# Edge attention on one Trainium2 core: the three logit products of a group on one column tile or on three

## What is computed

```
q, v = node_h @ Wq.T + bq, node_h @ Wv.T + bv          # 6250 x 8 heads x 16
k    = edge_attr @ Wk.T + bk                           # 100000 x 8 x 16
qs, qd = q[src], q[dst]
in_m, out_m, diag_m = sum(qs*k), sum(qd*k), sum(qs*qd) # over the 16 of a head
att   = distance ** lam
score = (seg_softmax(in_m/4, dst) + seg_softmax(out_m/4, dst) + seg_softmax(diag_m/4, dst)) * att
h     = segment_sum(score * v[dst], dst)
out   = leaky_relu(h @ Wo.T + bo, 0.1)
```

## Time and profile before

| | before |
|---|---|
| median of 3 runs | 7518.55 us (7517.9 to 7519.48) |
| the profiled execution | 7519.79 us |
| its span in the trace | 7518.0 us |
| PE busy | 5718.0 us (76%) |
| POOL busy | 5039.7 us (67%) |
| DVE busy | 3806.6 us (51%) |
| ACT busy | 1181.4 us (16%) |
| first and last logit product | 4785.2 and 6232.5 us |

### The profile page before, as it was taken

How to read it: one execution, slowest core, us unless ns; L and a number is a source line. 1 busy time by engine, 2 the same in 40 slices (tenths; PEclk the granted TensorE clock), 3 DMA queues, 4 the chain that set the end, 5 groups by cost and what they waited for, 6 DMA issues and landing times.

```text
span 7518.0 us, 99962 instructions
## 1 busy us (share of the span) xinstructions
PE 5718.0 (76%) x30467; PEld 3476.1 (46%) x30467; DVE 3806.6 (51%) x12655; ACT 1181.4 (16%) x3122; POOL 5039.7 (67%) x5069
## 2 busy tenths in 40 slices
PE   0677777777777777777577777899999995677776
PEld 0444444444444444444344444455555553444444
DVE  8834444444444444444544444577777777433335
ACT  0600000000000000000100000466666664000000
POOL 7077777677777677777577776466666661677774
PEclk9599999999999999999899999999999997999999
DMA  1021111211111211111111111354555450111111
GB/s 49 20 62 53 53 53 53 60 53 53 53 53 53 60 54 53 53 53 53 55 53 53 53 53 48 100 124 120 124 125 122 122 124 20 55 53 53 53 53 51
DMA packets 393953, 491.18 MB, mean 65 GB/s; under 512 B 104941, under 2 KB 291215, under 8 KB 393403
## 3 DMA queue, kind: packets, MB, share of 16 engines
q0 software_dynamic: 160528, 330.23, 15.7%
q1 hardware_dynamic: 229723, 153.27, 8.2%
q10 hardware_dynamic: 3168, 1.31, 0.1%
HBM read 459.92 MB, written 26.88 MB: 65 GB/s over the span
## 4 chain that ended last, share of the span: by engine, by line
POOL 52%; PE 22%; issue 17%; DVE 6%; ACT 1%; DMA 1%; ACTq 0%; DVEq 0%; POOLq 0%; SPq 0%
POOL pool L623 52%; PE psum L790 8%; PE psum L813 3%; PE psum L779 3%; PE psum L772 2%; DVE pool L1217 2%; PE psum L656 1%; PE psum L765 1%; PE psum L758 1%; PE psum L801 1%; PE psum L736 1%; PE psum L722 0%; DVE hot L1309 0%; DVE work L1051 0%; ACT work L929 0%
## 5 line engine op out<-in xcount | busy, mean ns | idle before, releaser
L623 POOL DMA_INDIRECT pool<-table,src_col x4160 | 3933.6, 946 | 1440.4 <-issue 1265.9
L745 PE MATMUL psum<-busy_rows,iota_b 128*128 128x512 bf16 x12480 | 3393.0, 381 | 0.0
L747 PE MATMUL psum<-pool 128*128 128x128 f32 x8320 | 1714.3, 288 | 1380.4 <-DVE pool L1342 1380.4
L747 PEld LDWEIGHTS psum<-pool 128*128 128x128 f32 x8320 | 1503.7, 191 | 2346.8 <-DVE pool L1342 1894.2
L1342 DVE TENSOR_SCALAR pool<-iota_f,rel_col,ew_col 128x128 f32<-128x128 f32 x3328 | 1228.5, 374 | 2291.4 <-DMA pool<-table,src_col 2290.4
L745 PEld LDWEIGHTS psum<-busy_rows,iota_b 128*128 128x128 bf16 x12480 | 1235.2, 99 | 545.9 <-issue 9.0
L1353 DVE TENSOR_TENSOR work<-work,psum 128x128 f32 x4160 | 1190.1, 286 | 252.6 <-PE psum L747 224.2
L605 POOL DMA_INDIRECT gath<-table,src_col x832 | 909.4, 1093 | 535.7 <-PE psum L765 341.2
L942 ACT ACTIVATE pool<-psum 128x512 f32<-128x512 f32 (+1 forms) x130 | 72.1, 566 | 4278.8 <-PE psum L722 4278.7
L790 PE MATMUL psum<-pool,head_sum 128*32 128x512 f32 x1248 | 614.9, 602 | 0.0
L1342 DVE TENSOR_SCALAR pool<-iota_f,rel_col 128x128 f32<-128x128 f32 x832 | 238.5, 287 | 577.6 <-DMA pool<-table,src_col 577.0
(11 more groups left out here) (195 smaller groups left out, 3938.6 us busy)
## 6 DMA issues: line engine op xcount, KB each, us to landing
pool<-table,src_col POOLq DMA_INDIRECT x4160, 2.5
pool<-edge_attr SPq DMA_DIRECT2D x832, 64.0 KB
pool<-step_masks SPq DMA_DIRECT2D x208, 192.0 KB
pool<-rel_rows SPq DMA_DIRECT2D x208, 128.0 KB, 3.1
table<-work SPq DMA_DIRECT2D x60, 256.0 KB, 2.3
gath<-table,src_col POOLq DMA_INDIRECT x832, 3.3
table<-QV SPq DMA_DIRECT2D x12, 256.0 KB, 2.3
out<-X SPq DMA_DIRECT2D x12, 256.0 KB
```

The lines of the kernel that those rows point to most:

```text
L623: gp.indirect_dma_start(out=gath_ring[:, s % RING, :], out_offset=None, in_=source[:, :], in_offset=bass.IndirectOffsetOnAxis(ap=src_col[: ...
L745: pe.matmul(psum[:, SUM_BANKS, :], iota_b[:, :], busy_rows[:, :], start=True, stop=True)
L747: pe.matmul(psum[:, s % SUM_BANKS, 0:D], hot_ring[:, s % HOT_RING, :], gath_ring[:, s % RING, :], start=True, stop=True).then_inc(steps.pr ...
```

## The change

The three kinds go to three column tiles, at partitions 0, 32 and 64 of the bank, and the quarters to eight rows each inside every tile: quarter q has the columns 8q to 8q + 7 of `head_sum`, and the four groups of a round accumulate into the same 96 rows. `keys(g + 1)` stands behind all three products instead of before the third, and PE waits for all three prods before the first. The logits signal once a group. Everything that worked on 128 partitions of the softmax works on 96, the ends are turned 96 columns wide and copied as 288, and a round's masks come in twelve loads of eight partitions, not four of 32.

```diff
-        head_sum = sb("head_sum", [P, 3, 32])
+        head_sum = sb("head_sum", [P, 4, 32])
...
-        ends = take(2, 3 * P)
+        KINDS = 3
+        ROWS = 32 * KINDS
+        ends = take(2, 3 * ROWS)
...
                 for q in range(QUADS):
                     s0 = q * QS + r * GROUP
-                    sp.dma_start(masks[32 * q:32 * (q + 1), r % 2, :, :],
-                                 spread(step_masks[:, s0:s0 + GROUP, :].rearrange("k (a s) e -> a k (s e)", a=1), 0, 32)
-                                 ).then_inc(masks_here[r % 2], 16)
+                    rows = step_masks[:, s0:s0 + GROUP, :].rearrange("k (a s) e -> a k (s e)", a=1)
+                    for kind in range(KINDS):
+                        first = 32 * kind + HEADS * q
+                        sp.dma_start(masks[first:first + HEADS, r % 2, :, :],
+                                     spread(rows, 0, HEADS)).then_inc(masks_here[r % 2], 16)
...
-            for k in range(3):
-                part = head_sum[:, k, HEADS * k:HEADS * (k + 1)]
+            for q in range(QUADS):
+                part = head_sum[:, q, HEADS * q:HEADS * (q + 1)]
...
-                for n, k in enumerate((2, 0, 1)):
-                    if n == 2 and g + 1 < NG:
-                        keys(g + 1)
-                    pe.wait_ge(prods_made, 3 * g + n + 1)
-                    pe.matmul(psum[32 * q:32 * (q + 1), bank, :], head_sum[:, k, :], prod[:, k, :], start=(n == 0),
-                              stop=(n == 2), tile_position=(0, 32 * q)).then_inc(logits_added, 1)
+                pe.wait_ge(prods_made, KINDS * (g + 1))
+                for kind in range(KINDS):
+                    ins = pe.matmul(psum[32 * kind:32 * (kind + 1), bank, :], head_sum[:, q, :], prod[:, kind, :],
+                                    start=(q == 0), stop=(q == QUADS - 1), tile_position=(0, 32 * kind))
+                ins.then_inc(logits_added, 1)
+                if g + 1 < NG:
+                    keys(g + 1)
...
-                for k, run in enumerate((m_run[:, cur, 1:BANK + 1], den_run[:, cur, :], num_run[:, cur, :])):
-                    ins = pe.transpose(psum[:, B_END, k * P:(k + 1) * P], run[:, j * P:(j + 1) * P], ident[:, :])
+                for k, run in enumerate((m_run[0:ROWS, cur, 1:BANK + 1], den_run[0:ROWS, cur, :], num_run[0:ROWS, cur, :])):
+                    ins = pe.transpose(psum[:, B_END, k * ROWS:(k + 1) * ROWS], run[:, j * P:(j + 1) * P], ident[0:ROWS, 0:ROWS])
...
-                values = ends[:, two, :].rearrange("p (k q c) -> p k q c", k=3, q=QUADS)
+                values = ends[:, two, :].rearrange("p (k i q h) -> p k i q h", k=3, i=KINDS, q=QUADS)
...
-                    ins = pe.matmul(psum[:, B_SUM, q * ACCW:(q + 1) * ACCW].rearrange("p (k c) -> p k c", k=3),
-                                    hot[:, two * QUADS + q, :], values[:, :, q, 0:SOFT], start=True, stop=True)
+                    ins = pe.matmul(psum[:, B_SUM, q * ACCW:(q + 1) * ACCW].rearrange("p (k i h) -> p k i h", k=3, i=KINDS),
+                                    hot[:, two * QUADS + q, :], values[:, :, :, q, :], start=True, stop=True)
...
-                act.activation(ends[:, c % 2, :], psum[:, B_END, 0:3 * P], ACT.Copy).then_inc(ends_copied, 1)
+                act.activation(ends[:, c % 2, :], psum[:, B_END, 0:3 * ROWS], ACT.Copy).then_inc(ends_copied, 1)
...
-                    v.wait_ge(logits_added, 3 * g)
+                    v.wait_ge(logits_added, g)
...
-                    v.wait_ge(logits_added, 3 * QUADS * (r + 1))
-                    v.wait_ge(masks_here[cur], 64 * (r // 2 + 1))
-                    v.tensor_tensor(invalid, psum[:, B_LOGIT[cur], :], invalid, ALU.add).then_inc(logits_masked, 1)
+                    v.wait_ge(logits_added, QUADS * (r + 1))
+                    v.wait_ge(masks_here[cur], 16 * QUADS * KINDS * (r // 2 + 1))
+                    v.tensor_tensor(invalid, psum[0:ROWS, B_LOGIT[cur], :], invalid, ALU.add).then_inc(logits_masked, 1)
```

More of the change, by code:

```diff
@@ L818, in attention_tensor @@
             pe.wait_ge(runs_clear, 3)
-            pe.wait_ge(head_sum_made, 10)
+            pe.wait_ge(head_sum_made, 1 + 3 * QUADS)
             turn_group(0)
@@ L994, in softmax_exp @@
             def softmax_exp(r, part):
-                starts = masks[:, r % 2, 1, :]
+                starts = masks[0:ROWS, r % 2, 1, :]
                 if part == 1:
                     act.wait_ge(below_made, r + 1)
-                    act.activation(expo[:, 0, :], expo[:, 0, :], ACT.Exp).then_inc(exp_made, 1)
+                    act.activation(expo[0:ROWS, 0, :], expo[0:ROWS, 0, :], ACT.Exp).then_inc(exp_made, 1)
                 else:
@@ L1385, in softmax_part @@
                 cur, old = r % 2, 1 - r % 2
-                m_now, m_before = m_run[:, cur, 1:BANK + 1], m_run[:, cur, 0:BANK]
-                invalid, starts, factor = (masks[:, cur, k, :] for k in range(3))
+                m_now, m_before = m_run[0:ROWS, cur, 1:BANK + 1], m_run[0:ROWS, cur, 0:BANK]
+                invalid, starts, factor = (masks[0:ROWS, cur, k, :] for k in range(3))
                 if part == 0:
-                    v.wait_ge(logits_added, 3 * QUADS * (r + 1))
-                    v.wait_ge(masks_here[cur], 64 * (r // 2 + 1))
-                    v.tensor_tensor(invalid, psum[:, B_LOGIT[cur], :], invalid, ALU.add).then_inc(logits_masked, 1)
+                    v.wait_ge(logits_added, QUADS * (r + 1))
+                    v.wait_ge(masks_here[cur], 16 * QUADS * KINDS * (r // 2 + 1))
+                    v.tensor_tensor(invalid, psum[0:ROWS, B_LOGIT[cur], :], invalid, ALU.add).then_inc(logits_masked, 1)
                     if r >= 2:
                         v.wait_ge(runs_turned, GROUP * (r - 1))
-                    v.tensor_copy(m_run[:, cur, 0:1], m_run[:, old, BANK:BANK + 1]).then_inc(own.up(), 1)
+                    v.tensor_copy(m_run[0:ROWS, cur, 0:1], m_run[0:ROWS, old, BANK:BANK + 1]).then_inc(own.up(), 1)
                     settle(own.value)
                     v.wait_ge(logits_masked, r + 1)
-                    v.tensor_tensor_scan(m_now, starts, invalid, m_run[:, cur, 0:1], ALU.add, ALU.max).then_inc(own.up(), 1)
+                    v.tensor_tensor_scan(m_now, starts, invalid, m_run[0:ROWS, cur, 0:1], ALU.add, ALU.max).then_inc(own.up(), 1)
                     soft["m"] = own.value
@@ L1400, in softmax_part @@
                     settle(soft["m"])
-                    v.tensor_tensor(expo[:, 0, :], invalid, m_now, ALU.subtract).then_inc(below_made, 1)
+                    v.tensor_tensor(expo[0:ROWS, 0, :], invalid, m_now, ALU.subtract).then_inc(below_made, 1)
                     v.tensor_tensor(starts, m_before, starts, ALU.add).then_inc(own.up(), 1)
@@ L1407, in softmax_part @@
                     v.wait_ge(exp_made, r + 1)
-                    v.tensor_tensor(factor, expo[:, 0, :], factor, ALU.mult).then_inc(own.up(), 1)
+                    v.tensor_tensor(factor, expo[0:ROWS, 0, :], factor, ALU.mult).then_inc(own.up(), 1)
                     soft["weighted"] = own.value
@@ L1411, in softmax_part @@
                     v.wait_ge(carry_made, r + 1)
-                    v.tensor_tensor_scan(den_run[:, cur, :], starts, expo[:, 0, :], den_run[:, old, BANK - 1:BANK], ALU.mult,
+                    v.tensor_tensor_scan(den_run[0:ROWS, cur, :], starts, expo[0:ROWS, 0, :], den_run[0:ROWS, old, BANK - 1:BANK], ALU.mult,
                                          ALU.add).then_inc(own.up(), 1)
                     settle(soft["weighted"])
-                    v.tensor_tensor_scan(num_run[:, cur, :], starts, factor, num_run[:, old, BANK - 1:BANK], ALU.mult,
+                    v.tensor_tensor_scan(num_run[0:ROWS, cur, :], starts, factor, num_run[0:ROWS, old, BANK - 1:BANK], ALU.mult,
                                          ALU.add).then_inc(num_made, 1)
```

## The result

The changed kernel takes 7241.21 us, the median of 4 runs (7238.71 to 7244.49), the kernel before 7518.9 beside it: 0.9631 of it, 95% interval 0.9614 to 0.9648. It is faster by 278 us. The forecast, 7293, is 52 us above it; the range, 7215 to 7475, holds it, and rival A's 7230 is the nearest of the recorded times.

The account below looks back on a forecast made before the run. PE was taken to bound the attention at 7.00 us a group, falling to 5.88: 199 x (7.00 - 5.88) = 223, and 4 for the first nine groups, 227 us off 7519.8 gives 7293 us; range 7215 to 7475.

Parts of the forecast that it names:

- rival A: Logit products: three tiles fully overlap, 0.97 us; POOL then binds at 5.61 us a group; 7230 us, chance 0.12.
- main term: Logit products on three column tiles: 2.80 us down to 1.83, saving 0.97 us a group on PE.
- the block is not four slots: Sign against the forecast: the six logit-product instructions on PE do not take four slots, 1.83 us.
- part 4: Next bound in the attention: DVE's prods have 1.3 us slack, POOL binds 0.27 us below 5.88, DMA engines about 0.56.
- part 1: Logit products on three column tiles: issue in written order gives four slots, 1.83 us, saving 0.97 us a group.
- Part 2: Keys behind the logits: two tile/full-array changes go, 0.11 us at the third product and 0.15 at keys to ends_sum.
- Part 3: 96 instead of 128: end transposes save between 0 and 0.08 us, taken as 0; ACT and DVE gain nothing.
- no PE idle over 0.1 us: Expected profile sign: PE never idles over 0.1 us in the middle of the attention.
- Part 5: Twelve mask issues a round on SP: 5.2 us, at least 6 us free before use, so nobody waits; cost nothing.
- rival D: SP's mask issues, x us each, make L515 land late and PE wait; decides at x = 0.7; slower, chance 0.07.

Follow-up runs that it names:

- e2: Changed kernel with logit kinds 0 and 2 on column tile 0 and kind 1 on tile 1 (time only): 7279.68 us, 0.9673 of the kernel before.
- e3: Kernel before with only keys(g + 1) moved behind the third logit product: 7458.17 us, 0.9908 of the kernel before.
- e10: Changed kernel without the fourth gather of each group, from the third group on (time only): 7168.30 us, 0.9527 of the kernel before.
- e4: Changed kernel with masks loaded in the first two rounds only: 7226.04 us, 0.9602 of the kernel before.
- e1: Changed kernel with all three logit products on column tile 0, same 32 rows (time only): 7440.85 us, 0.9887 of the kernel before.
- its three variants: Changed kernel with masks in four 24-partition loads, masks in two portions, or gathers without bounds check: 0.9887, 0.9910, 0.9899 of the kernel before (8539.79 us).

## Why the prediction was right, and where it was off

**Faster, inside the range: right,** with the main term mis-sized. By its own sign ("wrong if the block is not four slots") the mechanism that it chose failed, and the time came near for another reason: PE's work fell by 2.09 us a group where 1.12 was forecast, and POOL's floor, named in part 4 as thin cover, hid nearly all of the difference. That the miss shows as 52 us and not as 200 is luck for this forecast; only rival A had counted on that floor. The bound now (PE alone) and the worth of a microsecond off it were right as far as POOL's 5.61.

**The step that failed is part 1's choice of value:** "If products start in the order written, b of tile 0 waits 0.43 us for a, a of tile 1 stands behind it". It doesn't stand behind it: the block is 0.99 us, the lower end (0.97), not 1.83. The order holds within a tile only: the starts of the six instructions (three, then three) and e2's loads (four at once, then one by one) show it. e2's 1.84 us alone doesn't, since an issue in the order written would give four slots there too. The trace before couldn't show that, but 1.83 was an inference from one tile's behaviour to several.

The rule in the Trainium skill (TensorE: Matmul & The Clock Gate, Part 3, The mechanism) that a load overlaps a running product only when the row group differs is not borne out here: six loads with one and the same row group are done in 0.15 us, under the products of other tiles. The 2.38 times of its Measured speedup vs the span model for three column tiles is low for this kernel: 2.69 / 0.99 = 2.7.

**Part 2** took 0.11 + 0.15 = 0.26 us; e3 shows 0.31. **Part 3** took nothing for the transposes; they give 0.04. ACT and DVE gained nothing, as forecast: DVE's mean is 890 / 178 = 5.0 us.

**Part 4** was right in the two places that matter most: DVE waits for the keys, 20.1 us in 1000, and PE never for the prods in that stretch; and "0.27 us below 5.88 POOL binds" is what happened. That is rival A with its mechanism and its price (5.61 a group; measured 5.65), given a chance of 0.12. Part 4's share of the DMA engines was too low: 0.56 forecast, 0.64 measured at 5.62 us a group, though the masks are a quarter smaller. And "no PE idle over 0.1 us" failed: PE waits up to 3.2 us at a time.

**Part 5** had the issue time (5.2 us forecast, 4.15 to 4.6 measured, x = 0.35) but not the room. "At least 6 us are free" used a landing of 3.3 us, that of a gather, and groups of 5.88 us; behind the burst, attributes land after 5.2 to 6.9 us in e10 and up to 8.5 in the chain of the kernel after, the DMA engines are full (1.01 in the stage shown), and PE's own pace between two stalls is 4.9 us a group. So rival D's mechanism is there, at a small price: e4 puts it at 15 to 22 us, and with fewer gathers (e10) PE waits for attributes longer.

**Where the rest of PE's gain went.** 2.09 us a group, 435 us, came off PE; 278 were kept. The difference, 0.74 us a group, is POOL's floor (5.60 less 4.91 = 0.69) and the stalls above it (0.05).

## What to carry to other kernels

Products that use 32 output columns can run side by side (here six instructions took 0.99 us for 2.69): put those that are ready together on different column tiles, all of them between one change from full array to tiles and back, since each such change costs a weight load that nothing hides (0.1 to 0.2 us here). Before counting such a gain, add up the next engine's busy and issue time per unit of work: here it gave the new time of a group to 1%. Count a gather by its mean beside the work of the other engines, not by its best. And when the bound moves to a queue, look at bursts in front of it: twelve small issues once a round cost nothing while PE had 6.6 us of work a group (e1, PE busy 1000 of 1000 us), and show once it has 4.9.

## What the runs showed of the hardware that was not expected

- FP32 products of 128 x 32 by 128 x 512 on one, two and three column tiles: 2.69, 1.84 and 0.99 us for the same six instructions. Across three tiles three instructions start within 0.02 us, the other three 0.45 us later.
- After 3.5 us of waiting (5132.6 to 5136.4 us) the granted clock was 0.57 in the 4 us that followed, so mostly 1.2 GHz, and the logit products took 0.87 us more than at 2.4 GHz.
- The kernel before took 7518 to 7526 us on some chips and 8540 on another, with gathers of the same length; the changed kernel gained 3.7% on the former, and its three variants near 1% on the latter. Whether the chip or the moment made this, no run tells.
- The bounds check of an indirect gather is 0.05 us of POOL's time (0.999 and 0.947 us, medians).
- An indirect gather took 1.01 us on average away from four softmax lines of DVE, and beside them 1.38 us in the kernel after and 1.48 in the kernel before. No run tested the cause.
